# Regrouping the ranked tiles of a two-layer graph kernel: five groups in place of four, and their records written ahead

## The reference

```python
# layer 0
h = relu(layernorm(x))
H = h @ W.T + b;  s = H @ a_s;  r = H @ a_r
e = leaky_relu(A * s + A * r.T, 0.2)
x = x + softmax(where(A > 0, e, -9e15), axis=1) @ H
# layer 1
h = relu(layernorm(x)) @ weight
out = relu(adj @ h + bias)
x = x + max over neighbours j of out[j]        # _graph_pool
```

## Time and profile before

| | before |
|---|---|
| median of 3 runs | 2622.08 us (2621.01 to 2623.65) |
| the profiled execution's own time | 2613.49 us |
| its span | 2611.7 us |
| POOL busy | 1420.8 us (54%), 1465 instructions |
| DVE busy | 1495.5 us (57%) |
| PE busy | 1286.9 us (49%) |
| ACT busy | 464.7 us (18%) |
| mean granted TensorE clock | 0.732 |

### The profile page before, as it was taken

How to read it: one execution, slowest core, us unless ns; L and a number is a source line. 1 busy time by engine, 2 the same in 40 slices (tenths; PEclk the granted TensorE clock), 3 DMA queues, 4 the chain that set the end, 5 groups by cost and what they waited for, 6 DMA issues and landing times.

```text
span 2611.7 us, 18582 instructions
## 1 busy us (share of the span) xinstructions
PE 1286.9 (49%) x5093; PEld 672.1 (26%) x5093; DVE 1495.5 (57%) x3498; ACT 464.7 (18%) x1561; POOL 1420.8 (54%) x1465
## 2 busy tenths in 40 slices
PE   3764245635243636533556996951532212475046
PEld 1441024413132313322442442420211101232013
DVE  6988757967343625437155553544757754883234
ACT  1641134502122403451440000000000000000000
POOL 0012655562755463568536556357757775567763
PEclk8987567867576767765777998975776555787568
DMA  9999848789674879842343222114212321222221
GB/s 357 404 375 413 279 146 297 292 281 356 219 299 141 312 275 398 334 158 56 95 130 90 60 78 67 28 50 89 51 46 68 91 76 36 55 53 51 72 69 44
DMA packets 161754, 443.40 MB, mean 170 GB/s; under 512 B 31986, under 2 KB 90661, under 8 KB 128750
## 3 DMA queue, kind: packets, MB, share of 16 engines
q1 hardware_dynamic: 78974, 307.90, 31.0%
q0 software_dynamic: 49360, 108.63, 16.6%
q10 hardware_dynamic: 33312, 25.63, 3.2%
HBM read 404.00 MB, written 37.98 MB: 169 GB/s over the span
## 4 chain that ended last, share of the span: by engine, by line
another core or an unknown queue 21%; PE 20%; DVE 16%; issue 14%; POOL 11%; DMA 7%; ACT 6%; SPq 5%; ACTq 0%; DVEq 0%; POOLq 0%
PE psV L1211 10%; DMA a_buf<-in_adj 6%; POOL ring L759 6%; POOL rec_all L759 5%; PE psV L1038 3%; SPq L480 2%; PE psH L1094 2%; ACT ring L851 2%; SPq L493 2%; PE psV L1232 2%; DVE a_buf L1677 2%; DVE a_buf L1680 1%; DVE trec L1485 1%; DVE V L1670 1%
## 5 line engine op out<-in xcount | busy, mean ns | idle before, releaser
L685 POOL DMA_INDIRECT ring<-h_table,srec x505 | 493.9, 978 | 280.7 <-issue 150.9
L1038 PE MATMUL psV<-a_buf,bit_ident 128*128 128x512 bf16 x1024 | 320.7, 479 | 215.5 <-DMA a_buf<-in_adj 155.2
L759 POOL DMA_INDIRECT rec_all<-p_table,srec x325 | 321.8, 990 | 184.4 <-issue 98.2
L1232 PE MATMUL psV<-a_buf,trec 128*128 128x512 f32 (+1 forms) x398 | 235.4, 746 | 249.4 <-issue 126.3
L1211 PE MATMUL psV<-rec_all,a_buf 128*128 128x512 bf16 x888 | 212.0, 393 | 51.1 <-issue 50.6
L1094 PE MATMUL psH<-ring,ident 128*128 128x128 f32 x1010 | 162.6, 324 | 142.6 <-issue 100.6
L1038 PEld LDWEIGHTS psV<-a_buf,bit_ident 128*128 128x128 bf16 x1024 | 116.0, 116 | 402.6 <-issue 292.5
L718 POOL DMA_INDIRECT ring<-y_table,srec x191 | 185.0, 969 | 60.9 <-issue 60.6
L1094 PEld LDWEIGHTS psH<-ring,ident 128*128 128x128 f32 x1010 | 154.4, 237 | 155.0 <-issue 145.3
L1232 PEld LDWEIGHTS psV<-a_buf,trec 128*128 128x128 f32 x398 | 94.5, 245 | 386.6 <-issue 243.2
L1232 PE MATMUL psH<-a_buf,trec 128*128 128x512 f32 x124 | 79.9, 778 | 216.5 <-issue 116.6
(11 more groups left out here) (258 smaller groups left out, 2296.2 us busy)
## 6 DMA issues: line engine op xcount, KB each, us to landing
a_buf<-in_adj SPq DMA_DIRECT2D x256, 1024.0 KB
ring<-h_table,srec POOLq DMA_INDIRECT x505
trec<-records ACTq DMA_DIRECT2D x63, 128.0 KB
packed<-wbuf ACTq DMA_DIRECT2D x28, 256.0 KB
a_buf<-packed SPq DMA_DIRECT2D x7, 1024.0 KB
rec_all<-p_table,srec POOLq DMA_INDIRECT x325
h_table<-stage POOLq DMA_DIRECT2D x16, 258.0 KB, 8.1
a_buf<-r_row SPq DMA_DIRECT2D x1, 4096.0 KB
```

The costliest lines, as they stand in the source:

```text
L685: pool.indirect_dma_start(ring[:, A_AT[q] + j, :], None, h_table, bass.IndirectOffsetOnAxis(srec_u[g][:, i, LIST + j:LIST + j + 1], 0)).th ...
L759: pool.indirect_dma_start(ring[:, at + j, 0:D] if at < RING else side[:, at - RING + j, :], None, p_table, bass.IndirectOffsetOnAxis(slot, ...
L1038: last = pe.matmul(psV[n % 2][:, h * BANK:(h + 1) * BANK].rearrange("p (g n) -> p g n", n=P), bit_ident[:, k, :], rows[:, :, k, :], start= ...
L1232: pe.matmul(psO[b % len(psO)][:, 0:width], results[:, n % RESULTS, :], hot[:, c % HOT, at:at + width], start=(ranked_tile(n) == FIRST[g]), ...
```

## The change

The four groups become five: the third is cut from 20 to 16 tiles, and the last 20 tiles become groups of 12 and 8. The slots are 131, 183, 93, 63 and 43, 513 in all. In the second group the widest tile (41 slots) is processed last instead of first. POOL no longer writes a group's records directly ahead of its gathers: the record scatters stand five tiles ahead (`RANK_BEHIND`), the list load three ahead (`LIST_BEHIND`), and only the wait for the lists stays at the group's first tile. `STEP`, `BEHIND`, `LOADS` and `SPLIT_LAST` are new, and the overflow tile covers five first tiles with 25 rows each instead of four with 32. Buffers are laid out anew so that a fifth group's records lie beside saved rows.

```diff
-GROUPS = [(12, 16, 24), (1, 11, 48), (28, 20, 24), (48, 16, 16)]
+GROUPS = [(12, 16, 24), (1, 11, 48), (28, 16, 24), (44, 12, 16), (56, 8, 16)]
...
-         [14, 9, 8, 8, 7, 7, 6, 6, 6, 5, 5, 5, 5, 4, 4, 4, 3, 3, 2, 2],
-         [14, 8, 7, 6, 6, 5, 5, 4, 4, 4, 3, 3, 3, 2, 2, 2]]
-RANKED = [(g, i, k) for g in range(4) for i, k in enumerate(SLOTS[g])]
+         [14, 9, 8, 7, 7, 6, 6, 6, 5, 5, 4, 4, 4, 3, 3, 2],
+         [13, 8, 7, 6, 5, 5, 4, 4, 3, 3, 3, 2],
+         [14, 6, 6, 5, 4, 3, 3, 2]]
+
+ORDER = [list(range(n)) for _, n, _ in GROUPS]
+ORDER[1] = list(range(1, 11)) + [0]
+RANKED = [(g, i, SLOTS[g][i]) for g in range(NG) for i in ORDER[g]]
...
-LOADS = [15, 22, 40, 56]
+LOADS = [15, 22, 38, 50, 61]
+RANK_BEHIND = [FIRST[g] - 5 for g in range(1, NG)]
+LIST_BEHIND = [FIRST[g] - 3 for g in range(1, NG)]
...
-WIDE = [14, 31, 11, 9]
+WIDE = [15, 32, 11, 10, 8]
...
-STEP = [18, 19, 20, 20, 21, 22, 22, 23, 24, 24, 25, 25, 26, 26, 27, 27, 34, 38, 40, 41, 42, 43, 44, 45, 46, 46,
-    47, 53, 54, 55, 55, 56, 57, 57, 58, 58, 59, 60, 60, 61, 61, 62, 62, 63, 63, 64, 64, 65, 66, 67, 68, 68,
-    69, 69, 70, 70, 71, 71, 72, 72, 73, 73, 74]
-BEHIND = [5, 6, 8, 8, 9, 11, 11, 12, 14, 14, 16, 16, 17, 17, 17, 17, 20, 21, 23, 24, 25, 26, 27, 27, 30, 30, 31,
-    32, 33, 35, 35, 36, 38, 38, 40, 40, 41, 44, 44, 47, 47, 47, 47, 49, 49, 51, 51, 52, 53, 54, 56, 56, 58,
-    58, 61, 61, 62, 62, 62, 62, 62, 62, 62]
+STEP = [18, 19, 20, 20, 21, 22, 22, 23, 24, 24, 26, 26, 28, 29, 29, 30, 33, 35, 36, 37, 39, 40, 40, 45, 47, 48, 51, 52, 53, 54, 54, 55, 56, 56, 57, 57, 58, 59, 59, 60, 61, 61, 62, 63, 63, 64, 64, 65, 65, 66, 66, 67, 67, 68, 68, 69, 69, 70, 70, 71, 71, 72, 72]
+BEHIND = [6, 6, 6, 7, 8, 10, 11, 11, 11, 12, 13, 13, 16, 16, 16, 18, 18, 19, 23, 23, 23, 23, 23, 26, 26, 26, 29, 31, 33, 36, 36, 39, 39, 39, 39, 40, 40, 43, 43, 45, 46, 47, 47, 49, 49, 51, 52, 53, 53, 56, 56, 57, 57, 60, 60, 62, 62, 62, 62, 62, 62, 62, 62]
...
-SPLIT_LAST = {0: 46, 12: 62}
+SPLIT_LAST = {0: 42, 8: 54, 12: 62}
...
                     pool.indirect_dma_start(records[g], bass.IndirectOffsetOnAxis(rank[:, g, i:i + 1], 0),
                                             rec[g][:, i, :], None).then_inc(s_rec, 16)
+
+            def load_lists(g):
                 pool.wait_ge(s_rec, 16 * sum(m for _, m, _ in GROUPS[:g + 1]))
                 pool.dma_start(srec[g][:], records[g][:, LISTS:].rearrange("(t p) c -> p t c", p=P)).then_inc(
                     s_srec, 16)
-                pool.wait_ge(s_srec, 16 * (g + 1))
...
+            rank_group(0)
+            load_lists(0)
             for q in range(NR):
-                if RANKED[q][1] == 0:
-                    rank_group(RANKED[q][0])
+                if q in FIRST:
+                    pool.wait_ge(s_srec, 16 * (RANKED[q][0] + 1))
                 gather_h(q)
                 for m in SCATTER_BEHIND[q]:
                     scatter_y(m)
+                if q in RANK_BEHIND:
+                    rank_group(RANK_BEHIND.index(q) + 1)
+                if q in LIST_BEHIND:
+                    load_lists(LIST_BEHIND.index(q) + 1)
```

More of the change, by code:

```diff
@@ L36 @@
          [41, 24, 20, 17, 15, 14, 13, 12, 10, 9, 8],
[2 rows of a table removed]
-RANKED = [(g, i, k) for g in range(4) for i, k in enumerate(SLOTS[g])]
[3 rows of a table added]
+ORDER = [list(range(n)) for _, n, _ in GROUPS]
+ORDER[1] = list(range(1, 11)) + [0]
+RANKED = [(g, i, SLOTS[g][i]) for g in range(NG) for i in ORDER[g]]
+FIRST = [sum(n for _, n, _ in GROUPS[:g]) for g in range(NG)]
+TILE_SLOTS = [k for row in SLOTS for k in row]
 NR = len(RANKED)
-FIRST = [sum(n for _, n, _ in GROUPS[:g]) for g in range(NG)]
 STREAM = [t for a, n, _ in GROUPS for t in range(a, a + n)] + [0]
@@ L67 @@
 CHUNKS = 4
-ENDS = [sum(n for _, n, _ in GROUPS[:g + 1]) - 1 for g in range(4)]
-LOADS = [15, 22, 40, 56]
+ENDS = [sum(n for _, n, _ in GROUPS[:g + 1]) - 1 for g in range(NG)]
+LOADS = [15, 22, 38, 50, 61]
+RANK_BEHIND = [FIRST[g] - 5 for g in range(1, NG)]
+LIST_BEHIND = [FIRST[g] - 3 for g in range(1, NG)]
 RECORDS = 12
@@ L268, in build @@
         hub_in = [wbuf[:, i * WORDS:(i + 1) * WORDS] for i in range(2)]
-        rec_all = [sb(f"rec_all{i}", [P, max(n * (LISTS + LIST + w) for _, n, w in GROUPS[i::2])]) for i in range(2)]
-        rec = [rec_all[g % 2][:, 0:n * (LISTS + LIST + w)].rearrange("p (n c) -> p n c", n=n)
+        rec_words = [n * (LISTS + LIST + w) for _, n, w in GROUPS]
+        y_words = (NR - DENSE_FROM) * D
+        rec_at = [(sum(n for _, n, _ in GROUPS[:4]) - DENSE_FROM) * D if g == 4 else 0 for g in range(NG)]
+        rec_all = [sb("rec_all0", [P, max(rec_words[0], rec_words[2], y_words, rec_at[4] + rec_words[4])]),
+                   sb("rec_all1", [P, max(rec_words[1], rec_words[3], 4 * WORDS, SIDE * D)])]
+        rec = [rec_all[g % 2][:, rec_at[g]:rec_at[g] + n * (LISTS + LIST + w)].rearrange("p (n c) -> p n c", n=n)
                for g, (_, n, w) in enumerate(GROUPS)]
@@ L370, in build @@
         rank_f = sb("rank_f", [P, MOST])
-        rank = sb("rank", [P, 4, MOST], U32)
+        rank = sb("rank", [P, NG, MOST], U32)
         e_sc = [sb(f"e_sc{i}", [P, 49]) for i in range(2)]
@@ L408, in build @@
         over_rows = a_buf[:, 1, 0:OVER * D].rearrange("p (s d) -> p s d", d=D)
-        over_top = stage[0][0:TOP, :, 0:D]
+        over_top = [stage[g // BATCH][0:TOP, g % BATCH, 0:D] for g in range(NG)]
         turned_out = hT
@@ L577, in _ @@
             for g in range(len(GROUPS)):
-                sp.dma_start(over_top[:, g, :], over_max[g * TOP:(g + 1) * TOP, :]).then_inc(s_overtop, 16)
+                sp.dma_start(over_top[g], over_max[g * TOP:(g + 1) * TOP, :]).then_inc(s_overtop, 16)
             for c in range(2, PLANES):
@@ L820, in load_record @@
                 g, i, _ = RANKED[q]
-                if i == 0:
+                if q == FIRST[g]:
                     act.wait_ge(s_srec, 16 * (g + 1))
@@ L1182, in _ @@
                         pe.wait_ge(s_wt, DENSE)
-                        pe.wait_ge(s_onehot, 4)
+                        pe.wait_ge(s_onehot, NG)
                     for c in range(4 * (n - HUB_SUMS), 4 * (n - HUB_SUMS) + 4):
@@ L1277, in _ @@
             for q in range(NR):
-                dve.memset(slot_no[:, q:q + 1], float(A_SLOTS[q]))
+                dve.memset(slot_no[:, q:q + 1], float(TILE_SLOTS[q]))
             dve.drain()
@@ L1691, in join_top @@
                 dve.wait_ge(s_overtop, 16 * len(GROUPS))
-                return dve.tensor_tensor(row[0:TOP, :], row[0:TOP, :], over_top[:, g, :], ALU.max)
+                return dve.tensor_tensor(row[0:TOP, :], row[0:TOP, :], over_top[g], ALU.max)
             def best_of(n):
```

2 lines of the change are left out of this document (1 added, 1 removed).

## The result

| | before | after |
|---|---|---|
| median | 2621.55 us (2613.84 to 2623.65, 4 runs) | 2667.52 us (2663.30 to 2669.69, 4 runs) |
| ratio, 95% interval | | 1.0194 (1.0172 to 1.0217): slower |
| profiled execution (span) | 2613.49 us (2611.7) | 2669.69 us (2668.0) |

The forecast was 2520 us, faster, between 2450 and 2612. The kernel became 1.9% slower instead, and the interval of the ratio lies clear of 1.

The account below looks back on a forecast made before the run. POOL was taken to bound stages 1 (305 us idle) and 3, PE stage 2. Stage 1 -74, stage 2 0, stage 3 -14, the end -14 sum to -102: 2511.5 us profiled, median 2520, range 2450 to 2612.

Parts of the forecast that it names:

- the first: Stage 1, up to the y gathers: the new order cuts POOL's waits, 1093 to 1019 us, -74.
- The ring wait of 51.6: Second group: POOL's wait until the 41-slot tile was summed; it and the other ring waits, 75 us, would go.
- the second term that failed: Stage 2: PE's stage, matmuls unchanged, eight more POOL gathers hidden in idle time; 0, bounds -30 and +20.
- stage 3: From the first overflow gather: six more gathers +8, a quarter of the waits on DVE, 22, saved; -14.
- The cover named: Stage 2: POOL is not busy for 173 of 395 us, so eight more gathers (10 us) cost nothing.
- First group: Stage 1, first group: two more scatters inside it, rank wait at its twelfth tile; 256 us, 15 less to 25 more.
- Rival D: Slower: six of steps 33 to 42 crawl at 41 us beside 115 unbroken gathers, 25 us each; 2670 us; chance 0.12.
- Rival C: Waits only change their name: rank, 41-slot tile and row waits return 43 us, stage 3 10; 2593 us; chance 0.24.

Follow-up runs that it names:

- e11: Kernel after the change with every layer-1 row scatter two tiles later in POOL's order (BEHIND plus 2, at most 62); 2688.66 us, ratio 1.0273.
- e17: Kernel after the change, unedited, run again in a job without the crawl; 2299.00 us, ratio 1.0150 to before.
- e13: Kernel after, but the fifth group's first ranked tile gathers 6 of its 14 slots in stages 1 and 2; 2281.97 us, ratio 1.0093.
- e14: Kernel after with one slot fewer in the second to ninth tiles of the third group, all three stages; 2266.26 us, ratio 1.0013.
- e7: Kernel before with only the five groups, without the first 27 tiles' new order and tables or early records; 2665.57 us, ratio 1.0160.
- e5: Kernel after with POOL pausing ahead of every twelfth gather until landings, in the first 27 ranked tiles alone; 2677.65 us, ratio 1.0217.
- e8: Kernel after with pauses for landings ahead of every sixteenth gather in stage 3 and none in stage 1; 2665.36 us, ratio 1.0180.
- e16: e15 with pauses in the first 23 ranked tiles alone; 2343.89 us, ratio 1.0355 to before.
- e1: Kernel after with POOL pausing ahead of every twelfth gather of stage 1 until the gathers sent have landed; 2675.54 us, ratio 1.0197.
- e4: Kernel after with record scatters and list loads put back to the end of the group before; 2693.51 us, ratio 1.0267.
- e9: Kernel after with SLOTS itself cut to 6 for the fifth group's first ranked tile; its dense fallback ran, 303028.54 us.
- e12: e6 with pauses in 26 tiles, none in the 41-slot tile; 2616.17 us, ratio 0.9999 to before.
- e18: The kernel of e14 once more, in one job with e17; 2267.91 us, ratio 1.0020 to before.
- e6: Kernel before with after's order, early records and tables for the first 27 tiles, plus pauses every twelfth gather there; 2618.29 us, ratio 0.9988.
- e15: e12 with the row scatters of ranked tiles 23 to 25 one tile later (BEHIND 27 for 26); 2341.60 us, ratio 1.0348 to before.

## Why the forecast was wrong

- **The step that failed is the first: that 305 us of POOL's waits in stage 1 are time which a better order gets back** (-74; it came to +37, 1093 to 1130). Much of it is not time of the order but of slow steps. The four largest of after add to 322 us (215.2 + 71.0 + 20.0 + 15.9), the three largest of the same kernel without the crawl to 113 (55.9 + 38.2 + 18.7). The ring wait of 51.6 went as forecast, and the time went to ranks and rows. e11 shows the exchange with the order alone: 142 us fewer for rows, 153 more for ranks and ring, stage 1 18 us longer.
- **Gathers costed too low.** Stage 1's eight were in the sum (10 us). Stage 2's eight, the second term that failed, were costed at 0 since POOL had idle time; they cost 12 (e17 against e13 and e14), and with the crawl the stage grew by 19. In stage 3 I let 22 us of waits for DVE go; before's 86 became 96 (51.2 + 30.3 + 14.0), and the six gathers (+8) stood: 833 instead of 807. 22 gathers at 1.30 are 29 us, some three fifths of the 46 lost; that is an estimate, since the 1.30 was measured without the crawl, and e13 shows that a gather can also cost next to nothing. The cover named ("POOL is not busy for 173 us") was no cover: POOL spends the time in waits for DVE's sums (112.0 us after, 47.0 in e17), and the new gathers did not fit into them. By what path DVE waits in turn was not followed.
- **First group:** the wait at the twelfth tile cost 15.1 us and the three row scatters bunched behind the seventh waited 22 (all waits for rows in this group were 39.6 us before and 38.3 after, so it is the wait for ranks, 1.9 before, that grew); 267 against 256, inside the bounds.
- **Rival D** gave 2670 us, with the crawl in the long run at the head of the second group; 2668 came. The kind was right, the place in part: one of the slow steps (39) lies between 33 and 42, the other two (30 and 49) before and behind, and they fell into runs of 55, 40 and 42 issues, not into one of 115; the price of a step was too low (33 to 41 us over the same steps of e17, not 25) and the number too high (three, not six). And before had its own steps of 41 to 51 us, so that only the difference counts. The total was right by luck: without any crawl the change still loses 1.5%. By the two ratios the crawl's own share is 0.44% or 12 us, and the two intervals touch at 1.0172, so it may be nothing. Its chance, 0.12, was too small: the rows of before showed it at its work, and I left it in the numbers that the sum started from.
- **Rival C**, that waits change their name only, had the mechanism that e11 shows, and stopped half way: it kept 11 us of gain in stage 1 and 18 behind it, and had no price for stage 2.
- The rule cited with D, that both kinds of DMA queue take turns on an engine (the Trainium skill, "DMA: Bandwidth & Descriptors", "SWDGE vs HWDGE vs iDMA"), does not explain the crawl: DVE waits 1 to 2.4 us for its own instruction, and in stage 3 the crawl lies in a stretch where DMA is busy 0.24 of the time.

**Left open:** of the 46 us, the part beyond the gathers and the 12 us; why e7 loses 42 where its gathers explain 29 (the stall in its step 62 was not tested); why eight gathers of the fifth group's first tile cost 1 us in stage 1 (e13) and eight of the third group 10 (e14); before's stages without the crawl (only its time was taken there); what the crawl is, the recording of updates included, and why one and the same kernel has it in some jobs and not in others.

## What to carry to other kernels

Two engines in lockstep wait for each other by turns; a sum over one engine's waits counts the same slowness under many names, and removing a name gained nothing here. Cost every instruction of the engine that sets such a loop at its full interval, even where it seems to have idle time: here 1.30 us a gather on the mean of three stages (but 1 us for eight where e13 took them out of stage 1). And before an order is changed to remove waits, look whether the steps waited for are slow by themselves (an engine late on its own signals), since then the order alone may not help. Compare, too, how many semaphore updates two traces of one program hold, before a late signal is put down to the program.

## What the runs showed of the hardware

- The crawl: in some jobs, while POOL issues indirect DMAs without a pause, signals between and within engines come 1 to 2.4 us late, from 12 to 30 us into the run (stage 1), and the trace holds 1.4 updates per us where it otherwise holds 14 to 19. Waiting for landings ahead of every twelfth gather takes away a good part of it (288 to 69 us in stage 1, or 348 to 248 by the wider count) and costs as much as it brings here.
- It does not come with the kernel alone: before took 2614 to 2623 us in three jobs and 2262 to 2263 in two, 14% less, where no stretch of crawl is found in the six profiles. The number of the chip in the records was the same (11) for e5 to e8, with it, and e13 to e16, without; e1 to e4 and e9 to e12 had 10, e17 and e18 had 13. Times of different jobs can't be compared; ratios within one can, and even these may depend on it: the four-group kernels with pauses stood level with before where there was the crawl (e6, e12) and 3.5% above it where there was none (e15, e16).
